# Second-layer attention: queries' rotary sum on POOL, one product per table place, row sums at other heads

## Chip, cores, metric

One core of one Trainium2 chip runs the whole program. The metric is device time in microseconds (us) of one execution, as the median of several. PE is TensorE, DVE is VectorE, ACT is ScalarE, POOL is GpSimd, SP is SyncE, which here only issues DMAs.

## What is computed

Two layers, each `x = x + s * silu(ffn)` with `s` an attention of the normalised input. The change touches only the second layer's attention and the routing work that runs beside it:

```python
# 4 sequences of 512 rows, 256 wide; 16 heads of 128; window 64
h = rmsnorm(layernorm(x)) * norm_w
Q, K, V = lora_proj(h, wq, ...), lora_proj(h, wk, ...), lora_proj(h, wv, ...)
Q = Q * cos + rotate_half(Q) * sin        # the same for K
attn = softmax(Q K^T / sqrt(128) + window mask)
s = lora_proj(attn V, wo, ...) + layernorm(x)
# second ffn: each row goes to 4 of 16 experts
topk_w, topk_ids = top_k(softmax(x @ gate_w.T), 4)
out = shared_expert(x) * sigmoid(...) + sum over the 4 of w * expert(x)
```

For the experts the kernel makes a table: 80 tiles of 128 places sorted by expert, and for each place which row (and which of its 4 choices) stands in it. 2048 rows x 4 choices = 8192 entries; they are brought to their places with one-hot products.

## The kernel before

The program runs in stages that all engines end together; the attention of the second layer is stage 4. There each engine runs its own loop over 64 heads (4 sequences x 16), written out by hand, and engines meet through semaphores. `upto(eng, s, k)` waits until step k of semaphore s was reported, `seen` does the same for counters without lead, and `then_inc` reports. Each engine takes its instructions in the order written.

In turn h of the loop, with the heads that the engines work on at the same time:

- **PE**: `project(h+2)` (L1001; queries, then keys), in some turns `turn_rows` of a tile, an output quarter of an earlier group (L1063), `scores(h+1)` (L1032), `attend(h-1)` (L1051), `turn_probs(h)` (L1041), `values` (L1014).
- **ACT**: `swap(h+2, 0)` and `swap(h+2, 1)` (L1382 and L1383: the rotated halves of queries and keys from PSUM), `output_high`, four exponentials (L1406), `probs_out`, `value_out`; in eight turns the table's L1463.
- **DVE**: `cosine(h+2)` twice (L1808, queries then keys), `masked(h+1)` (four L1828, each with a row minimum; before them, in some turns, the copy or sum of what the table's product left in PSUM), in every second turn `add_output` (L1856), `turned(h+2)` twice (L1814: cosine part + sine part, queries then keys), `output_low` (L1848), `inverse` (L1836), `probs_out` (L1842), and then the turn's extra work.
- **POOL**: `sine(h+2)` (L2166 twice, queries then keys), `normalized(h+1)` (two halves, L2173, then a drain that reports).

The extra work of DVE follows dictionaries of turns. `SUM_AT` says in which turn the first layer's rows of tile t are summed (`summed`: L1730, L1732, L1734, adding 8 loaded parts pairwise) and, one turn later, finished (`finish`: L1740, L1742, L1744, L1746). After the last tile of a sequence come its statistics, and `FOLLOW_AT`, worked out from `SUM_AT`, says in which turns the sequence's four tiles are normalised, turned by PE and split (`rows_low`, L1769). The table's steps run from turn `T0` (two after the last tile's follow-up): counting in `tables(k)`, then eight chunks of eight choices each in turns `T0 + 10` on (`chunk`), the products in `scores` from head `CHUNK0 + 1` on, and the end (from L1961) in turn `T0 + 11 + 8`.

`chunk(c)` makes a one-hot of the tile number for each of eight choices (`ohhi1`, L1891), multiplies it with a code of the column (`ohcol`, L1894), and makes a one-hot of the place in the tile (`ohlo1`, L1895). ACT makes a second scaled copy with the partition's number (`ohtok`, L1463). PE then makes two products for each choice, sixteen in a chunk (L1026 and L1028), all into one PSUM region, which `masked` adds to `idxf` (L1825). All second-layer tiles lie in one buffer called arena in the rows.

Of the kernel before, what the change touches and what calls it, by code (L numbers as in the profile page):

```python
# [8 lines left out]
F16 = mybir.dt.float16  # L9
# [6 lines left out]
P = 128  # L16
T = 2048
NB, SEQ, D = 4, 512, 256
NT = T // P
# [70 lines left out]
def build(nc, io, dbg):  # L90
    ctx = ExitStack()
    with ctx:
# [127 lines left out]
        class Landed:  # L220
# [65 lines left out]
        chosen, counted, counted_rd, exp5_in, exp5_done, chunk_in, tables_done = (  # L286
            sem(n) for n in ("chosen", "counted", "counted_rd", "exp5_in", "exp5_done", "chunk_in", "tables_done"))
# [8 lines left out]
        rope_done = loop_sem("rope_done", "dve", 1, AHEAD)  # L296
# [144 lines left out]
        at_cnt = R6.at  # L441
        CHUNK = 8
        NCHUNK = NT * K1 // CHUNK
        ohhi1 = R6.take(P, CHUNK, XT, dt=F16)
        R6.at = at_cnt
# [10 lines left out]
        colA = R6.take(P, NT * K1)  # L456
# [8 lines left out]
        ohtok = R6.take(P, 2, CHUNK, XT, dt=F16)  # L465
# [82 lines left out]
        SUM_AT = {4: 0, 5: 2, 6: 3, 7: 6, 8: 11, 9: 15, 10: 17, 11: 19, 12: 23, 13: 25, 14: 27, 15: 28}  # L548
# [243 lines left out]
        def _(pe):  # L792
# [225 lines left out]
            def scores(h, u):  # L1018
                upto(pe, sm_done, h - 1)
                for t in tiles_at(FOLLOW_AT, h - 3):  # L1020
                    router(t, ps[4][:, 2 * KW:2 * KW + E1 + 1])
                if 0 <= h - 1 - CHUNK0 < NCHUNK:
                    c = h - 1 - CHUNK0
                    seen(pe, chunk_in, c)
# [198 lines left out]
        def _(act):  # L1223
# [154 lines left out]
            def swap(h, s):  # L1378
                k = 2 * h + s
                upto(act, cos_rd, k)  # L1380
                upto(act, rope_done, k - 2)
                nc.scalar.activation(qk_s[0:64, s], ps[s][64:P, :], ACT.Copy)  # L1382
                nc.scalar.activation(qk_s[64:P, s], ps[s][0:64, :], ACT.Copy).then_inc(swap_rd, 1)  # L1383
# [41 lines left out]
            for h in range(NH):  # L1425
# [108 lines left out]
        def _(dve):  # L1534
# [270 lines left out]
            def cosine(h, s):  # L1805
                upto(dve, proj_mm, 2 * h + s)
                upto(dve, rope_done, 2 * h + s - 2)
# [51 lines left out]
            for h in range(2):  # L1859
                cosine(h, 0)  # L1860
                cosine(h, 1)
                turned(h, h, 0)
                turned(h, h, 1)
# [23 lines left out]
            def chunk(c):  # L1887

                at = slice(CHUNK * c, CHUNK * (c + 1))
                seen(dve, chunk_in, c - 1)  # L1890
# [7 lines left out]
            def tables(k):  # L1898
# [48 lines left out]
                if k == 9:  # L1947
# [6 lines left out]
                    nc.vector.tensor_scalar(colA, iota[:, 0:NT * K1], 1.0, float(P), ALU.add, ALU.mult)  # L1954
                    dve.drain()
                    nc.vector.tensor_copy(loA, loI)
# [23 lines left out]
            for h in range(NH):  # L1980
# [18 lines left out]
                if ahead:  # L1999
                    turned(h + 2, h % 2, 0)  # L2000
                    turned(h + 2, h % 2, 1)
# [106 lines left out]
        def _(pool):  # L2108
# [130 lines left out]
```

## Time and profile before

| | us |
|---|---|
| median of 3 runs | 1355.68 (1355.54 to 1359.92) |
| the profiled execution | 1360.36 |
| its span, first to last instruction | 1358.2 |
| of it, the 64 heads of stage 4 | some 610 |

The profile is one execution. Busy time counts work on an engine; L12 is line 12 of the kernel before. "Idle before" names what ended an engine's wait. `x2` in a timeline row means that two instructions are merged in it. In the chain of waits, "issue" is time in which the engine waited for nothing that the profile shows.

### The profile page before, as it was taken

To read this page: it belongs to the slowest core of one execution; us is meant where nothing else is said; L and a number is where in the kernel's file an instruction comes from. 1 tells how busy PE (TensorE), PEld (TensorE's weight loads), DVE (VectorE), ACT (ScalarE), POOL (GpSimd) and SP (SyncE) were. 2 spreads that over 40 slices of the span, in tenths; PEclk is the share of its full clock that TensorE was granted. 3 is DMA by queue.
4 is the path that set the end of the run, shared out by engine and by line. 5 is a ranking of instruction groups with operands and counts; after the bars stand their busy time and mean duration, and the time that the engine had idled before them with its cause. 6 is when DMAs were issued, how large, how long until landed. Compare 5 with 4: busy or idle time off the path is not lost.

```text
span 1358.2 us, 21102 instructions
## 1 busy us (share of the span) xinstructions
PE 1120.9 (83%) x6075; PEld 709.8 (52%) x6075; DVE 887.2 (65%) x2124; ACT 634.9 (47%) x1680; POOL 600.3 (44%) x577
## 2 busy tenths in 40 slices
PE   4967898617888897887898888898878889788998
PEld 3545343214556665665675555567545455445454
DVE  4586166754887789888777999987443333333575
ACT  1532244434568655855866455566333333333211
POOL 0485365303555454543544544455135565665100
PEclk8978898958999999999999999999888898998999
DMA  9692898580221213120110000020642222222261
GB/s 347 245 322 81 235 275 261 201 275 26 94 93 40 86 32 124 47 78 32 55 41 32 32 1 32 32 96 0 221 105 70 77 73 72 78 81 58 72 204 50
DMA packets 90170, 148.64 MB, mean 109 GB/s; under 512 B 11146, under 2 KB 61965, under 8 KB 87248
## 3 DMA queue, kind: packets, MB, share of 16 engines
q1 hardware_dynamic: 79312, 119.02, 26.4%
q0 software_dynamic: 10752, 28.33, 6.7%
q8 instruction: 52, 0.85, 0.3%
q14 instruction: 54, 0.44, 0.1%
HBM read 104.25 MB, written 45.15 MB: 110 GB/s over the span
## 4 chain that ended last, share of the span: by engine, by line
PE 40%; DVE 18%; issue 13%; ACT 7%; POOL 6%; DMA 4%; another core or an unknown queue 4%; DVEq 3%; ACTq 2%; POOLq 1%; SPq 1%; PEld 0%
PE ps L1173 5%; POOL arena L2166 4%; PE ps L1185 3%; PE ps L1001 3%; PE ps L1183 3%; PE ps L1063 2%; PE ps L822 2%; ACT arena L1383 2%; PE ps L1115 2%; PE ps L884 2%; DVE arena L1842 2%; PE ps L1032 2%; DVE arena L1814 2%; PE ps L1133 2%
## 5 line engine op out<-in xcount | busy, mean ns | idle before, releaser
L2166 POOL TENSOR_TENSOR arena<-arena 128x512 f32<-128x512 f32 x128 | 161.5, 1278 | 226.0 <-ACT arena L1383 225.8
L2173 POOL TENSOR_TENSOR arena<-arena 64x512 f32<-64x512 f32 x128 | 149.7, 1169 | 144.8 <-DVE arena L1836 141.1
L1001 PE MATMUL ps<-arena 128*128 128x512 f16 x768 | 182.1, 388 | 35.3 <-ACT arena L1383 35.3
L1814 DVE TENSOR_TENSOR arena<-arena 128x512 f32<-128x512 f32 x128 | 126.6, 1025 | 33.2 <-POOL arena L2166 31.3
L1001 PEld LDWEIGHTS ps<-arena 128*128 128x128 f16 x768 | 74.1, 99 | 135.7 <-ACT arena L1383 45.5
L2194 POOL DMA_INDIRECT z_d<-wvo,put x80 | 80.9, 1011 | 91.4 <-DVE wvo L2058 69.7
L1382 ACT ACTIVATE arena<-ps 64x512 f32<-64x512 f32 x128 | 76.1, 595 | 93.6 <-DVE arena L1808 89.8
L1406 ACT ACTIVATE arena<-arena 128x192 f32<-128x192 f32 x256 | 112.6, 444 | 2.4 <-DVEq L1831 2.4
L2190 POOL DMA_INDIRECT wvo<-xn_d,idx x80 | 78.0, 975 | 72.3 <-PE ps L1167 35.6
L1063 PE MATMUL ps<-wvo,arena 128*128 128x256 f16 x768 | 97.2, 279 | 13.3 <-DVE arena L1848 12.9
L1014 PE MATMUL ps<-wvo,arena 128*128 128x512 f16 x384 | 94.3, 382 | 16.3 <-ACTq L1361 9.1
L1032 PE MATMUL ps<-arena 128*128 128x192 f32 x512 | 96.3, 331 | 5.6 <-DVE arena L1814 3.8
L1063 PEld LDWEIGHTS ps<-wvo,arena 128*128 128x128 f16 x768 | 75.9, 100 | 35.5 <-DVE arena L1848 17.7
L1173 PE MATMUL ps<-arena,wvo 128*128 x480 | 93.4, 336 | 0.4 <-issue 0.4
L1808 DVE TENSOR_TENSOR arena<-ps,wvo 128x512 f32<-128x512 f32 x128 | 82.8, 681 | 12.6 <-PE ps L1001 10.7
L1051 PE MATMUL ps<-arena 128*128 128x192 f32 (+1 forms) x512 | 87.5, 314 | 4.0 <-DVE arena L1842 4.0
L1828 DVE CUSTOM_DVE_ANT_0 arena<-ps,arena 128x192 f32<-128x192 f32 x256 | 75.7, 351 | 21.7 <-PE ps L1032 21.7
L1051 PEld LDWEIGHTS ps<-arena 128*128 128x128 f32 x512 | 84.8, 190 | 4.8 <-issue 2.5
L1032 PEld LDWEIGHTS ps<-arena 128*128 128x128 f32 x512 | 82.5, 191 | 8.5 <-issue 5.5
L1183 PE MATMUL ps<-arena,wvo 128*128 x160 | 54.7, 426 | 38.8 <-ACTq L1503 38.8
L2044 DVE SCALAR_TENSOR_TENSOR wvo<-ps,wvo 128x256 f16<-128x256 f32 x80 | 34.0, 425 | 75.7 <-ACT wvo L1491 62.2
L1383 ACT ACTIVATE arena<-ps 64x512 f32<-64x512 f32 x128 | 75.5, 590 | 1.5
(286 smaller groups left out, 2205.4 us busy)
## 6 DMA issues: line engine op xcount, KB each, us to landing
arena<-z_d SPq DMA_DIRECT2D x16, 1024.0 KB, 5.9
arena<-wqk_d SPq DMA_DIRECT2D x16, 1024.0 KB, 5.0
arena<-in_wgu SPq DMA_DIRECT2D x32, 384.0 KB
z_d<-wvo SPq DMA_DIRECT2D x8, 1024.0 KB, 4.2
z_d<-wvo SPq DMA_DIRECT2D x2, 4096.0 KB, 25.8
wvo<-z_d SPq DMA_DIRECT2D x16, 512.0 KB, 5.0
arena<-in_wdn SPq DMA_DIRECT2D x32, 192.0 KB
arena<-in_w13T SPq DMA_DIRECT2D x4, 1408.0 KB, 13.1
```

What stands on the lines that cost most here:

```text
L1001: last = pe.matmul(ps[s][:, :], wqk[gg][:, s * DC + c, w, hh * DH:(hh + 1) * DH], hx[bb][:, :, x, c * P:(c + 1) * P], start=(c == 0 and w ...
L1014: last = pe.matmul(ps[2][:, :], hx[bb][:, q, x, c * P:(c + 1) * P], wvo16[:, UNITS + c * NG + g, w], start=(c == 0 and w == x), stop=(c == ...
L1032: last = pe.matmul(ps[3 + q // 2][:, (q % 2) * KW:(q % 2 + 1) * KW], qr[:, u, q * P:(q + 1) * P], kr[:, u, q * P:q * P + KW], start=True, ...
L1051: last = pe.matmul(ps[7][:, k * P:k * P + n], vv[gg][:, k, hh * DH:(hh + 1) * DH], flat(pT[:, k])[:, 0:n], start=(k == 0), stop=(k == TPB ...
L1063: last = pe.matmul(output_bank(n, half)[:, q % 2 * D:(q % 2 + 1) * D], oT[gg][:, x, hh, q * P:(q + 1) * P], wvo16[:, 2 * g + hh // 2, w, h ...
L1173: last = pe.matmul(ps[bank][:, 0:2 * F1], lhs[:, x, c * P:(c + 1) * P], w13[:, bass.ds(e, 1), w, c * 2 * F1:(c + 1) * 2 * F1].rearrange("p ...
L1183: pe.matmul(ps[bank][:, 0:D], h1T[:, u, 0:P], w2a[:, bass.ds(e, 1), :].rearrange("p a d -> p (a d)"), start=start, stop=False)
L1383: nc.scalar.activation(qk_s[64:P, s], ps[s][0:64, :], ACT.Copy).then_inc(swap_rd, 1)
L1406: nc.scalar.activation(pp[u][:, q], sm[:, q], ACT.Exp, bias=mn[:, q:q + 1], scale=-1.0, accum_out=rs[:, q:q + 1])
L1814: nc.vector.tensor_tensor(dst, qk_c[:, s], qk_s[:, s], ALU.add).then_inc(rope_done, 1)
L2166: nc.gpsimd.tensor_tensor(qk_s[:, s], qk_s[:, s], sin, ALU.mult).then_inc(sin_done, 1)
L2173: nc.gpsimd.tensor_tensor(pm[u][rows, at:at + SEQ].rearrange("p (t n) -> p t n", t=TPB), pp[u][rows, :, at:at + P], ri[rows].unsqueeze(2). ...
```

## The change

It has three parts.

1. The sum of cosine part and sine part of the queries is issued by POOL, behind the two sines of that head. DVE keeps the keys' sum and waits for the sine of the keys before it. `rope_done` becomes two semaphores. `normalized` begins with a drain on POOL.
2. In a chunk of the table, eight `tensor_scalar` (one for each choice) compare with the tile number and multiply with a code that holds column and partition in one; the code is the same for each chunk. `ohhi1`, `ohtok`, ACT's L1463 and the second product are gone. What depends on the chunk is added in `masked` through `later`.
3. `SUM_AT` has other turns, and with it `FOLLOW_AT`, `T0` (36 before, 34 after) and `CHUNK0` (48, 46).

```diff
-        SUM_AT = {4: 0, 5: 2, 6: 3, 7: 6, 8: 11, 9: 15, 10: 17, 11: 19, 12: 23, 13: 25, 14: 27, 15: 28}
+        SUM_AT = {4: 0, 5: 2, 6: 4, 7: 6, 8: 9, 9: 11, 10: 13, 11: 15, 12: 17, 13: 22, 14: 24, 15: 26}
...
                     for i in range(CHUNK):
-                        pe.matmul(ps[4][:, 2 * KW:2 * KW + XT], ohlo1[:, c % 2, i], ohtok[:, c % 2, i], start=(i == 0), stop=False,
+                        pe.matmul(ps[4][:, 2 * KW:2 * KW + XT], ohlo1[:, c % 2, i], ohcol[:, c % 2, i], start=(i == 0), stop=(i == CHUNK - 1),
                                   skip_group_check=True)
-                        pe.matmul(ps[4][:, 2 * KW:2 * KW + XT], ohlo1[:, c % 2, i], ohcol[:, c % 2, i], start=False, stop=(i == CHUNK - 1),
-                                  skip_group_check=True)
-                upto(pe, rope_done, 2 * h + 1)
+                upto(pe, rope_done[0], h)
+                upto(pe, rope_done[1], h)
...
-                if 0 <= h - T0 - 10 < NCHUNK:
-                    c = h - T0 - 10
-                    act.wait_ge(picked, c + 1)
-                    nc.scalar.activation(flat(ohtok[:, c % 2]), flat(ohhi1), ACT.Copy, scale=pid[:, 0:1]).then_inc(chunk_in, 1)
...
-            def turned(h, u, s):
-                upto(dve, sin_done, 2 * h + s)
+            def turned(h, u):
+                upto(dve, sin_done, 2 * h + 1)
                 upto(dve, sc_ps, h - 2)
-                dst = qr[:, u] if s == 0 else kr[:, u, WIN:WIN + SEQ]
-                nc.vector.tensor_tensor(dst, qk_c[:, s], qk_s[:, s], ALU.add).then_inc(rope_done, 1)
+                nc.vector.tensor_tensor(kr[:, u, WIN:WIN + SEQ], qk_c[:, 1], qk_s[:, 1], ALU.add).then_inc(rope_done[1], 1)
...
                 if 0 < h - 1 - CHUNK0 < NCHUNK:
+                    c = h - 1 - CHUNK0
+                    nc.vector.tensor_scalar(later, ps[4][:, 2 * KW:2 * KW + XT], 0.0, float(CHUNK * P * c), ALU.is_gt, ALU.mult)
                     nc.vector.tensor_tensor(idxf, idxf, ps[4][:, 2 * KW:2 * KW + XT], ALU.add)
+                    dve.drain()
+                    nc.vector.tensor_tensor(idxf, idxf, later, ALU.add)
...
-                nc.vector.tensor_tensor(ohhi1, iota_bf[:, 0:XT].unsqueeze(1).to_broadcast([P, CHUNK, XT]),
-                                        hiA[:, at].unsqueeze(2).to_broadcast([P, CHUNK, XT]), ALU.is_equal)
-                dve.drain()
-                nc.vector.tensor_tensor(ohcol[:, c % 2], ohhi1, colA[:, at].unsqueeze(2).to_broadcast([P, CHUNK, XT]), ALU.mult)
+                for i in range(CHUNK):
+                    nc.vector.tensor_scalar(ohcol[:, c % 2, i], iota_bf[:, 0:XT], hiA[:, CHUNK * c + i:CHUNK * c + i + 1], colA[:, i:i + 1],
+                                            ALU.is_equal, ALU.mult)
...
                 for s in range(2):
                     upto(pool, swap_rd, 2 * h + s)
                     nc.gpsimd.tensor_tensor(qk_s[:, s], qk_s[:, s], sin, ALU.mult).then_inc(sin_done, 1)
+                upto(pool, sin_done, 2 * h)
+                upto(pool, cos_rd, 2 * h)
+                upto(pool, sc_ps, h - 2)
+                nc.gpsimd.tensor_tensor(qr[:, h % 2], qk_c[:, 0], qk_s[:, 0], ALU.add).then_inc(rope_done[0], 1)
 
             def normalized(h, u):
+                pool.drain()
                 upto(pool, rs_done, h)
```

## Rows read from the trace of the kernel before

**Rows 1.** The page, part 1: busy us, share of span, instructions

```profile
PE 1120.9 (83%) x6075; PEld 709.8 (52%) x6075; DVE 887.2 (65%) x2124; ACT 634.9 (47%) x1680; POOL 600.3 (44%) x577
```

**Rows 2.** Table by stretches: from:to, length, busy us of PE, PEld, DVE, ACT, POOL

```profile
332.00:942.00 610.00, 529.07 (x3253) 371.67 (x3252) 514.74 (x1235) 389.49 (x1011) 302.40 (x250) 0.99 0.16 53
```

**Rows 3.** The same table, stretches of two heads, one table head, one head

```profile
489.21:509.41 20.20, 18.76 (x116) 13.49 (x115) 18.70 (x40) 11.59 (x31) 10.12 (x8) 1.00 0.19 54
812.09:823.09 11.00, 7.54 (x59) 5.44 (x58) 10.60 (x22) 6.41 (x16) 5.06 (x4) 1.00 0.27 95
917.78:925.91 8.13, 8.13 (x52) 5.88 (x51) 5.26 (x17) 5.59 (x15) 4.70 (x5) 1.00 0.00 0
```

**Rows 4.** Chain of waits in order of time: start us, us, what

```profile
335.06 1.28 POOL arena L2166
...
344.85 1.28 POOL arena L2166
...
346.16 0.03 DVE arena L1814
...
347.83 0.62 DVE arena L1814
...
897.77 1.28 POOL arena L2166
```

**Rows 5.** Groups by line, 332 to 942 us, DVE: count, busy us, mean ns, idle

```profile
L1814 DVE TENSOR_TENSOR arena<-arena 128x512 f32<-128x512 f32 x124 | 122.8, 1027 | 30.0 <-POOL arena L2166 28.1 <-issue 0.9
L1808 DVE TENSOR_TENSOR arena<-ps,wvo 128x512 f32<-128x512 f32 x124 | 80.1, 681 | 3.8 <-PE ps L1001 2.5 <-issue 0.7
```

**Rows 6.** Timeline: start us, us, engine, line, what, xcount merged

```profile
491.18 2.50 POOL L2166 TENSOR_TENSOR arena<-arena 128x512 f32<-128x512 f32 x2 [2.96 <-ACT arena L1383]
...
492.48 2.34 DVE L1814 TENSOR_TENSOR arena<-arena 128x512 f32<-128x512 f32 x2
...
498.66 0.43 DVE L1746 BATCH_NORM_STATS2 stat<-x_sb 128x6 f32<-128x256 f32 x1
...
499.01 1.27 DVE L1808 TENSOR_TENSOR arena<-ps,wvo 128x512 f32<-128x512 f32 x2
...
911.67 2.50 POOL L2166 TENSOR_TENSOR arena<-arena 128x512 f32<-128x512 f32 x2 [0.53 <-ACT arena L1383]
...
914.96 1.28 DVE L1814 TENSOR_TENSOR arena<-arena 128x512 f32<-128x512 f32 x2
```

**Rows 7.** Timeline, a sine that began during a DVE add

```profile
455.47 1.64 POOL L2166 TENSOR_TENSOR arena<-arena 128x512 f32<-128x512 f32 x1 [0.98 <-ACT arena L1383]
```

**Rows 8.** Timeline of a table head

```profile
815.61 2.34 DVE L1814 TENSOR_TENSOR arena<-arena 128x512 f32<-128x512 f32 x2 [0.20 <-POOL arena L2166]
...
819.13 1.30 DVE L1891 TENSOR_TENSOR arena<-iota_bf,arena 128x640 f16<-128x640 bf16 x1
...
821.93 1.21 DVE L1895 TENSOR_TENSOR arena<-iota_bf,arena 128x1024 f16<-128x1024 bf16 x1
823.07 1.28 DVE L1808 TENSOR_TENSOR arena<-ps,wvo 128x512 f32<-128x512 f32 x2
...
825.30 2.49 POOL L2166 TENSOR_TENSOR arena<-arena 128x512 f32<-128x512 f32 x2 [3.98 <-ACT arena L1383]
```

**Rows 9.** Timeline, small DVE operations with one input

```profile
789.62 0.20 DVE L1952 TENSOR_SCALAR arena<-arena 128x64 int32<-128x64 int32 x1
789.73 0.19 DVE L1953 TENSOR_SCALAR arena<-arena 128x64 int32<-128x64 int32 x1
...
891.98 0.67 DVE L1961 TENSOR_SCALAR arena<-arena 128x80 int32<-128x80 f32 x1
```

**Rows 10.** Table by stretches: four heads; two with a sum; two without

```profile
353.90:393.24 39.34, 29.22 (x163) 19.44 (x164) 34.94 (x76) 23.19 (x63) 18.84 (x16) 1.00 0.25 81
442.40:463.72 21.32, 19.47 (x125) 14.41 (x125) 18.55 (x50) 11.68 (x32) 8.71 (x7) 1.00 0.26 81
665.71:685.26 19.55, 18.35 (x118) 13.49 (x117) 12.82 (x43) 13.91 (x36) 8.82 (x9) 1.00 0.26 81
```

More of the change, by code:

```diff
@@ L285, in build @@
         kept = [sem(f"kept{b}") for b in range(NB)]
-        chosen, counted, counted_rd, exp5_in, exp5_done, chunk_in, tables_done = (
-            sem(n) for n in ("chosen", "counted", "counted_rd", "exp5_in", "exp5_done", "chunk_in", "tables_done"))
+        chosen, counted, counted_rd, exp5_in, exp5_done, tables_done = (
+            sem(n) for n in ("chosen", "counted", "counted_rd", "exp5_in", "exp5_done", "tables_done"))
         tabs_in = sem("tabs_in")
@@ L295, in build @@
         sin_done = loop_sem("sin_done", "pool", 1, AHEAD)
-        rope_done = loop_sem("rope_done", "dve", 1, AHEAD)
+        rope_done = [loop_sem("rope_q", "pool", 1, AHEAD), loop_sem("rope_k", "dve", 1, AHEAD)]
         v_ps = loop_sem("v_ps", "pe", 1, AHEAD)
@@ L440, in build @@
         mkA = R6.take(P, NT, E1, dt=BF16)
-        at_cnt = R6.at
         CHUNK = 8
         NCHUNK = NT * K1 // CHUNK
-        ohhi1 = R6.take(P, CHUNK, XT, dt=F16)
-        R6.at = at_cnt
         cnt = [R6.take(P, NT, E1) for _ in range(3)]
@@ L455, in build @@
         hiA = R6.take(P, NT * K1)
-        colA = R6.take(P, NT * K1)
+        colA = R6.take(P, CHUNK)
+        later = R6.take(P, XT)
         etf = R6.take(1, XT)
@@ L464, in build @@
         ohlo1 = R6.take(P, 2, CHUNK, P, dt=F16)
-        ohtok = R6.take(P, 2, CHUNK, XT, dt=F16)
         ohcol = R6.take(P, 2, CHUNK, XT, dt=F16)
@@ L1023, in scores @@
                     c = h - 1 - CHUNK0
-                    seen(pe, chunk_in, c)
+                    seen(pe, picked, c)
                     for i in range(CHUNK):
-                        pe.matmul(ps[4][:, 2 * KW:2 * KW + XT], ohlo1[:, c % 2, i], ohtok[:, c % 2, i], start=(i == 0), stop=False,
+                        pe.matmul(ps[4][:, 2 * KW:2 * KW + XT], ohlo1[:, c % 2, i], ohcol[:, c % 2, i], start=(i == 0), stop=(i == CHUNK - 1),
                                   skip_group_check=True)
-                        pe.matmul(ps[4][:, 2 * KW:2 * KW + XT], ohlo1[:, c % 2, i], ohcol[:, c % 2, i], start=False, stop=(i == CHUNK - 1),
-                                  skip_group_check=True)
-                upto(pe, rope_done, 2 * h + 1)
+                upto(pe, rope_done[0], h)
+                upto(pe, rope_done[1], h)
                 for q in range(TPB):
@@ L1380, in swap @@
                 upto(act, cos_rd, k)
-                upto(act, rope_done, k - 2)
+                upto(act, rope_done[s], h - 1)
                 nc.scalar.activation(qk_s[0:64, s], ps[s][64:P, :], ACT.Copy)
@@ L1806, in cosine @@
                 upto(dve, proj_mm, 2 * h + s)
-                upto(dve, rope_done, 2 * h + s - 2)
+                upto(dve, rope_done[s], h - 1)
                 nc.vector.tensor_tensor(qk_c[:, s], ps[s][:, :], cos, ALU.mult).then_inc(cos_rd, 1)
-            def turned(h, u, s):
-                upto(dve, sin_done, 2 * h + s)
+            def turned(h, u):
+                upto(dve, sin_done, 2 * h + 1)
                 upto(dve, sc_ps, h - 2)
-                dst = qr[:, u] if s == 0 else kr[:, u, WIN:WIN + SEQ]
-                nc.vector.tensor_tensor(dst, qk_c[:, s], qk_s[:, s], ALU.add).then_inc(rope_done, 1)
+                nc.vector.tensor_tensor(kr[:, u, WIN:WIN + SEQ], qk_c[:, 1], qk_s[:, 1], ALU.add).then_inc(rope_done[1], 1)
             def masked(h):
@@ L1861, in _ @@
                 cosine(h, 1)
-                turned(h, h, 0)
-                turned(h, h, 1)
+                turned(h, h)
             masked(0)
@@ L1889, in chunk @@
                 at = slice(CHUNK * c, CHUNK * (c + 1))
-                seen(dve, chunk_in, c - 1)
-                nc.vector.tensor_tensor(ohhi1, iota_bf[:, 0:XT].unsqueeze(1).to_broadcast([P, CHUNK, XT]),
-                                        hiA[:, at].unsqueeze(2).to_broadcast([P, CHUNK, XT]), ALU.is_equal)
-                dve.drain()
-                nc.vector.tensor_tensor(ohcol[:, c % 2], ohhi1, colA[:, at].unsqueeze(2).to_broadcast([P, CHUNK, XT]), ALU.mult)
+                for i in range(CHUNK):
+                    nc.vector.tensor_scalar(ohcol[:, c % 2, i], iota_bf[:, 0:XT], hiA[:, CHUNK * c + i:CHUNK * c + i + 1], colA[:, i:i + 1],
+                                            ALU.is_equal, ALU.mult)
                 nc.vector.tensor_tensor(ohlo1[:, c % 2], iota_bf[:, :].unsqueeze(1).to_broadcast([P, CHUNK, P]),
@@ L1953, in tables @@
                     nc.vector.tensor_scalar(hiI, dstI, 7, None, ALU.arith_shift_right)
-                    nc.vector.tensor_scalar(colA, iota[:, 0:NT * K1], 1.0, float(P), ALU.add, ALU.mult)
+                    nc.vector.tensor_scalar(colA, iota[:, 0:CHUNK], 1.0, float(P), ALU.add, ALU.mult)
                     dve.drain()
+                    nc.vector.tensor_scalar(colA, colA, pid[:, 0:1], None, ALU.add)
                     nc.vector.tensor_copy(loA, loI)
@@ L1999, in _ @@
                 if ahead:
-                    turned(h + 2, h % 2, 0)
-                    turned(h + 2, h % 2, 1)
+                    turned(h + 2, h % 2)
                 if h:
```

## Prediction

> **What bounds the kernel now.** The parts of the page came first. PE is busy 83% of the span, but that is a mean over stages [rows 1]. The table by stretches cuts the span into stages: the stretch from 332 to 942 us is the 64 heads of the second layer's attention, the only stage the change touches. It has 610 us, DVE busy 515, PE 529, POOL 302 [rows 2]. Next came stretches of single heads, from one head's first L1808 (the cosine product) to the next's. A head with nothing extra takes 8.13 us, all of it PE: the floor. A head with a row sum and the one after it, which finishes the tile, take 20.20 together, 10.1 each; a head that builds table entries takes 11.0. There DVE is busy 18.70 of 20.20 and 10.60 of 11.00, and PE has gaps [rows 3].
>
> The chain of waits says what DVE waits for there. From the cosine product of the queries it goes DVE L1808, ACT L1382 and L1383 (the two swaps), POOL L2166 (sine of the queries), then DVE L1814, whose second of the pair ends at 347.83 + 0.62 = 348.45 [rows 4]. Behind it on DVE stand L1848, L1842, the tile's work and the next L1808. So the loop closes through DVE, and passes POOL once per head.
>
> The rows that decide are those of L1814. Undisturbed, a pair of them takes 1.28 us, so one takes about 0.68 with the overlap of 0.08 that the pair of L1808 (mean 0.681, same size) shows; but the mean of 124 is 1.027 [rows 5, 6]. (1.027 - 0.68) x 124 = 43 us are lost. A typical pair shows how: POOL's two sines run from 491.18 for 2.50, DVE's two adds start at 492.48 and take 2.34 instead of 1.28. The first add starts behind the first sine, finds POOL in its second sine, and ends about 0.5 after that one's end [rows 6]. L1808, which reads one input from PSUM, keeps 0.681 as a mean [rows 5]. So an add with both inputs in SBUF stands still while POOL works. With 1.06 us lost by each, 43 us is some 40 of 62 heads. It holds the other way too: the sine of 455.47 began while an add was already running, and took 1.64 rather than 1.28 [rows 4, 7].
>
> **Part 1, the queries' add goes to POOL.** DVE loses one L1814 a head, POOL gains one instruction. Its price on POOL is that of the sine, which has the same shape: 1.28 [rows 4]. POOL has room: 302 of 610 us, + 62 x 1.28 = 79. But DVE's remaining add (keys) must wait for the sine of the keys anyway. Call the end of that sine S and the query cosine's start C. In rows bound by DVE the pair before ends at S + 1.15: at 491.18 + 2.50 = 493.68 = S, the adds end at 492.48 + 2.34 = 494.82 [rows 6].
>
> After the change POOL has the queries' add queued directly behind the keys' sine. Its three waits (its own first sine, the cosine, the scores of two heads ago) are all met by then. Are they dealt with while the sine still runs? On DVE they are: L1746 starts at 498.66 and takes 0.43, three waits stand between it and L1808, and L1808 starts at 499.01, before its end [rows 6]. On POOL two sines together take 2.50 against 2 x 1.28, so the second starts some 0.05 before the end of the first, while DVE, which waits for a semaphore, starts 0.03 after it (344.85 + 1.28 = 346.13, L1814 at 346.16) [rows 4, 6]. So I take it that POOL gets in first. Then the keys' add stands still for 1.25 and needs its 0.5: it ends at S + 1.77, 0.62 later than before. The busy time of DVE falls, and its chain grows. In the language of the Trainium skill ("SBUF — State Buffer", "Who interferes with whom") the read port of POOL and of two-input VectorE instructions goes to whichever issues first, for the whole instruction; both orders in rows 6 and 7 agree.
>
> How many heads pay? Those where DVE stands waiting for POOL and the chain goes through the sine. I followed the chain from head to head: 36 sines of queries lie on it with this pattern, the first at 335.06, the last at 897.77 [rows 4]; 8 of these are table heads, counted in part 2. Of the other 28, 25 pay 0.62. In three (sum and row turning in one head) POOL had an idle stretch between the sines which an add used at full speed; there only the keys' add was left at S (the sine of 455.47 ends at 457.11), the pair ended at S + 0.72, and the price is 1.05 [rows 7]. Together 25 x 0.62 + 3 x 1.05 = **+18.7**. In heads at PE's floor DVE arrives after S (914.96 against 911.67 + 2.50 = 914.17) [rows 6]: the add is blocked there as well and ends at S + 1.77 = 915.94, where the pair ended at 916.24, all beside PE work: nothing. Bounds: 28 x -0.47 = -13 if DVE gets in first (below), 36 x 1.05 = +38 if every head pays the dear price.
>
> **Part 2, the table.** Eight heads. DVE loses L1891 and L1894, ACT loses L1463, PE eight of sixteen small products. L1891 takes 1.30 and is mostly standing, behind POOL's first half of L2173; L1894 stands behind the second. From the end of the keys' add (815.61 + 2.34 = 817.95) to the next L1808 (823.07) it is 5.12 us, of that 1.21 L1895 [rows 8]. Added: eight tensor_scalar of 128x80. Two such of 128x64 start 0.11 apart and take 0.20 each, so eight are 7 x 0.11 + 0.20 = 0.97. But they meet POOL's halves too: L1961, one SBUF input, 128x80, took 0.67 behind a half [rows 9]. L1891 ends at 820.43 and needs 0.5 behind POOL, so the first half ends 1.95 after the keys' add [rows 8]. Then either the whole burst and L1895 go through (1.95 + 0.97 + 1.1 = 4.0), or POOL's second half gets in between (+1.05: 5.05). I take 4.5, the middle. ACT's 0.83 delayed the swap: C to S was 4.72 (823.07 to 825.30 + 2.49) [rows 8], it becomes 4.47 as in sum heads (489.21, where the stretch of rows 3 begins with L1808, to 493.68). The head was 4.73 + 1.15 + 5.12 = 11.0; it becomes 4.47 + 1.77 + 4.5 = 10.74: 8 x -0.26 = **-2.1**; bounds 10.24 and 11.29, so -6 to +2.5. The Trainium skill ("VectorE: DVE Perf Modes", "Side-by-side") counts about 150 cycles of start and decode at 0.96 GHz for each instruction; by an estimate from that page eight cost 1.25 us rather than 0.97, and the sum would be 8 x 0.28 = 2.2 us higher. The row has them overlapping, and the row decides. The new product and add in the masking step, some 0.2 each by the tensor_scalar of rows 9, fall where DVE waits for S. PE's and ACT's savings are beside DVE's chain.
>
> **Part 3, the sums spaced.** All twelve stay. One alone costs 20.20 - 2 x 8.13 = 3.9 [rows 3]; one in heads that turn rows 21.32 - 19.55 = 1.8, since those wait anyway [rows 10]. Sums 5 and 6, adjacent, with the free head behind them took 39.34; spaced, the four heads would be twice 20.20 = 40.4: spacing costs 1.0 [rows 3, 10]. Before, sums 8, 12 and 13 lay among the turning heads; after, 8 and 9 do, and 12 at the edge: between 0 and +2. Sum **+2**, bounds -4 (8 and 9 wholly absorbed) and +4. The table starts two heads earlier; its heads were DVE-bound and stay so. Row loads are asked for two sums ahead, now an even 40 us.
>
> **Sum.** 18.7 - 2.1 + 2 = +18.6. The profiled execution took 1360.36 us (span 1358.2 and 2.2 around it), 4.7 over the median of 1355.68. 1360.36 + 18.6 = 1379.0, against the median **1374.3**. Own range of this case: 1362 (half the heads pay, part 2 at its best) to 1386.
>
> **Rivals.** *DVE gets in first* (ends faster). If POOL's three waits take more than about 0.1 us beyond the sine's end, DVE's add starts at S + 0.03 and ends at S + 0.68: 0.47 less than before, in 28 heads -13.2; table heads 4.47 + 0.68 + 4.5 = 9.65, 8 x -1.35 = -10.8; part 3 +2. 1355.7 - 22.0 = 1334. It turns on 0.1 us of order on one engine. Against it: the 0.05 overlap of sine pairs. 13%.
> *The extra is absorbed* (no difference). The chain in DVE heads has other members near: PE is busy 18.76 of 20.20 in them [rows 3]. If only a third of the 0.62 reaches the next head and parts 2 and 3 come to their best (-10): 6.2 - 6 - 4 + 1355.7 = 1352, or 1356 with part 3 at 0. Against it: the chain never leaves DVE, ACT and POOL in a sum head [rows 4]. 10%.
> *More than that*: POOL's L2173 halves come late as well and the tile's sums meet them: the dear price in all 36, 1355.7 + 38 + 2 = 1396. Against it: the query add ends 0.5 before the keys' add, L2173 waits for L1836 well after. 5%.
>
> **Chances.** Forecast 72%, the rivals 13, 10 and 5. Slower by over 0.3% (4 us, about what a measurement of this kernel can tell from no change): 76%; within: 8%; faster: 16%. Range: 1350 to 1387; out of it are the first rival and the last.
>
> **What would show it.** Right: the DVE add of keys has a mean near 1.5 us with a blocked form of 1.74, starting 0.03 after the second sine; POOL shows three instructions in a row of 3.75 together; a sum head takes 11.0 and its follower 10.4; DVE's busy time falls while the stretch grows. Wrong: the keys' add takes 0.68 and POOL's add is the one stretched to 1.6 to 1.9. Part 2: table heads at 10.3 if the burst holds, 11.3 if it is cut, and L1895 blocked or not says which. Part 3 is wrong if sums 8 and 9 cost nothing among the turning heads.

## The result and the profile after

Beside runs of the kernel before on the same chip (median 1357.8 us), the changed kernel takes 1394.58 us as a median of four (1390.53 to 1395.02): 1.026 of the time before, 95% interval 1.0225 to 1.0296. The forecast was slower, 1374.3 with a range of 1350 to 1387: the sign was right, the size half of what came, and the time lies above the range.

The page's part 1, then the table by stretches of the kernel after. Its columns are those of [rows 2]; the first line is the stretch of all heads (from the first masking instruction of head 0 to that of head 63), then a head with a row sum and the head that finishes it, four heads (10 to 13) at the first turned rows, and a table head. The last three columns are PE's mean granted clock, the busy share of the DMA engines and GB/s:

```profile
PE 1136.9 (82%) x6011; PEld 716.1 (51%) x6011; DVE 866.8 (62%) x2123; ACT 628.3 (45%) x1672; POOL 675.8 (49%) x641
```

```profile
330.51:976.77 646.26, 546.89 (x3197) 379.70 (x3198) 496.37 (x1246) 384.17 (x1008) 375.66 (x312) 0.97 0.15 50
599.08:610.07 10.99, 7.92 (x37) 5.19 (x36) 9.40 (x19) 5.58 (x15) 6.68 (x5) 0.85 0.29 97
610.07:620.50 10.43, 10.43 (x67) 7.90 (x66) 8.07 (x19) 6.00 (x16) 5.87 (x5) 0.99 0.00 1
430.92:441.72 10.80, 10.13 (x66) 7.65 (x64) 8.73 (x18) 5.91 (x17) 6.68 (x5) 1.00 0.00 1
441.72:454.17 12.45, 9.11 (x58) 6.67 (x58) 9.45 (x23) 8.43 (x21) 5.92 (x5) 1.00 0.55 190
454.17:466.58 12.41, 10.26 (x55) 6.62 (x54) 9.81 (x24) 7.35 (x20) 6.71 (x5) 0.86 0.04 6
466.58:479.30 12.72, 10.64 (x58) 6.96 (x58) 9.87 (x26) 6.97 (x18) 5.91 (x5) 0.87 0.37 119
849.83:861.18 11.35, 9.01 (x52) 7.09 (x53) 10.44 (x29) 5.58 (x16) 5.85 (x5) 0.85 0.27 92
```

The span grew from 1358.2 to 1392.4, by 34.2 us. Measured between the same two instructions, the heads took 612.80 before and 646.26 after: 33.5 of it. What lies ahead of them grew by 1.2, what lies behind them shrank by 0.4. DVE's busy time fell from 887.2 to 866.8, POOL's rose from 600.3 to 675.8 [rows 1]: the engine that the work was taken from did less, and the heads took longer.

The groups by line for the sines, the keys' sum and the queries' sum (count, busy us, mean ns, idle before):

```profile
L2158 POOL TENSOR_TENSOR arena<-arena 128x512 f32<-128x512 f32 x128 | 160.4, 1270 | 227.2 <-ACT arena L1379 226.9
L1805 DVE TENSOR_TENSOR arena<-arena 128x512 f32<-128x512 f32 x64 | 98.9, 1546 | 80.9 <-POOL arena L2158 80.4
L2162 POOL TENSOR_TENSOR arena<-arena 128x512 f32<-128x512 f32 x64 | 81.2, 1269 | 0.0
```

The mean of DVE's sum went from 1027 ns [rows 5] to 1546, while POOL's own stays at 1269, the price of a sine. The timeline of the sum head in the table above shows one of them:

```profile
601.05 2.50 POOL L2158 TENSOR_TENSOR arena<-arena 128x512 f32<-128x512 f32 x2 [3.58 <-ACT arena L1379]
...
603.50 1.27 POOL L2162 TENSOR_TENSOR arena<-arena 128x512 f32<-128x512 f32 x1
603.58 1.74 DVE L1805 TENSOR_TENSOR arena<-arena 128x512 f32<-128x512 f32 x1 [1.32 <-POOL arena L2158]
605.25 0.68 DVE L1843 SCALAR_TENSOR_TENSOR arena<-ps,arena 128x512 f16<-128x512 f32 x1
```

The sines end at 603.55 (S). POOL's next instruction begins 0.05 before that, DVE's, which waits for a semaphore, 0.03 after it. DVE's stands still until POOL is through and ends at 605.32, which is S + 1.77. The chain of waits of the same head closes through DVE, ACT and POOL as in [rows 4]:

```profile
600.39 0.60 ACT arena L1379
...
601.05 2.51 POOL arena L2158 x2
...
603.58 0.04 DVE arena L1805
...
606.01 0.57 DVE arena L1837
606.58 1.62 DVE arena L1722
...
608.28 1.38 DVE arena L1724
```

### The profile page after: what moved, and what is told of

Same layout as the page of the kernel before. It is cut to its first block, busy times and chain, and to the rows that moved or that the text cites. A ratio compares the mean times of both kernels' runs of the same rounds, so it can differ in the third digit from the quotient of the medians.

```text
span 1392.4 us, 21114 instructions
## 1 busy us (share of the span) xinstructions
PE 1136.9 (82%) x6011; PEld 716.1 (51%) x6011; DVE 866.8 (62%) x2123; ACT 628.3 (45%) x1672; POOL 675.8 (49%) x641
## 4 chain that ended last, share of the span: by engine, by line
PE 40%; DVE 18%; issue 12%; POOL 9%; ACT 5%; DMA 4%; DVEq 4%; another core or an unknown queue 4%; POOLq 2%; ACTq 1%; SPq 1%; PEld 0%
POOL arena L2158 7%; PE ps L1169 5%; PE ps L1181 4%; PE ps L998 3%; PE ps L1179 3%; PE ps L1059 2%; PE ps L819 2%; PE ps L1111 2%; PE ps L1028 2%; DVE arena L1800 2%; PE ps L1011 2%; ACT arena L1379 2%; PE ps L1129 2%; PE ps L881 2%
## 5 line engine op out<-in xcount | busy, mean ns | idle before, releaser
L2158 POOL TENSOR_TENSOR arena<-arena 128x512 f32<-128x512 f32 x128 | 160.4, 1270 | 227.2 <-ACT arena L1379 226.9
L998 PE MATMUL ps<-arena 128*128 128x512 f16 x768 | 185.5, 393 | 34.9 <-ACT arena L1379 34.7
L2170 POOL TENSOR_TENSOR arena<-arena 64x512 f32<-64x512 f32 x128 | 147.9, 1155 | 101.1 <-DVE arena L1831 97.3
L1805 DVE TENSOR_TENSOR arena<-arena 128x512 f32<-128x512 f32 x64 | 98.9, 1546 | 80.9 <-POOL arena L2158 80.4
L1378 ACT ACTIVATE arena<-ps 64x512 f32<-64x512 f32 x128 | 76.1, 595 | 154.6 <-DVE arena L1800 151.2
L1028 PE MATMUL ps<-arena 128*128 128x192 f32 x512 | 102.3, 346 | 12.8 <-DVE arena L1805 10.2
L1028 PEld LDWEIGHTS ps<-arena 128*128 128x128 f32 x512 | 87.7, 201 | 18.9 <-issue 15.2
L1047 PEld LDWEIGHTS ps<-arena 128*128 128x128 f32 x512 | 85.9, 193 | 3.0 <-DVE arena L1843 2.3
L2162 POOL TENSOR_TENSOR arena<-arena 128x512 f32<-128x512 f32 x64 | 81.2, 1269 | 0.0
```

The source lines that it names most:

```text
L998: last = pe.matmul(ps[s][:, :], wqk[gg][:, s * DC + c, w, hh * DH:(hh + 1) * DH], hx[bb][:, :, x, c * P:(c + 1) * P], start=(c == 0 and w ...
L1047: last = pe.matmul(ps[7][:, k * P:k * P + n], vv[gg][:, k, hh * DH:(hh + 1) * DH], flat(pT[:, k])[:, 0:n], start=(k == 0), stop=(k == TPB ...
L1805: nc.vector.tensor_tensor(kr[:, u, WIN:WIN + SEQ], qk_c[:, 1], qk_s[:, 1], ALU.add).then_inc(rope_done[1], 1)
L2170: nc.gpsimd.tensor_tensor(pm[u][rows, at:at + SEQ].rearrange("p (t n) -> p t n", t=TPB), pp[u][rows, :, at:at + P], ri[rows].unsqueeze(2). ...
```

## The experiments

They ran on three chips on which the kernel before takes 1286.60, 1287.47 and 1286.72 us. The 70 us to the first chip lie outside the heads (in the kernels profiled there about 315 us ahead of them instead of 329, about 357 behind them instead of 416), and single heads untouched by an edit have the same length to 0.01. So each run is read twice: as a ratio, which compares medians on one chip, and as the length of the stretch of heads in its one profiled execution, against 612.80 in that of the kernel before.

The second reading has a scatter. The whole change was profiled twice, and its heads take 646.26 and 643.20: head 20 is 11.82 at a mean granted clock of 0.86 in the one and 10.25 at 1.00 in the other, head 29 is 9.79 and 8.12. So a difference of up to 3 us in the heads says little unless single heads show where it lies.

| kernel | us | ratio, 95% interval | heads | against before |
|---|---|---|---|---|
| part 1 alone | 1313.94 | 1.0208 (1.0191 to 1.0225) | 640.38 | +27.6 |
| part 2 alone | 1283.23 | 0.9976 (0.9967 to 0.9986) | 610.59 | -2.2 |
| part 3 alone | 1294.79 | 1.0071 (1.0047 to 1.0095) | 618.78 | +6.0 |
| parts 2 and 3 | 1290.85 | 1.0031 (1.0019 to 1.0042) | 618.96 | +6.2 |
| the whole change | 1317.66 | 1.0245 (1.0228 to 1.0263) | 643.20 | +30.4 |
| part 1, POOL's add after DVE's | 1292.86 | 1.0044 (1.0027 to 1.0062) | 619.63 | +6.8 |
| DVE adds queries, POOL keys | 1284.84 | 0.9983 (0.9969 to 0.9998) | 613.39 | +0.6 |
| part 1, half an add on POOL | 1294.65, one run | | 616.84 | +4.0 |
| part 1, POOL's add behind the halves | 1365.28 | 1.0625 (1.0602 to 1.0649) | 686.19 | +73.4 |
| two sums moved | 1285.63, one run | | 614.76 | +2.0 |
| part 3, swaps ahead of the copies | 1297.65 | 1.0084 (1.0057 to 1.0111) | 623.63 | +10.8 |
| part 2 with the other split | 1283.13 | 0.9973 (0.9962 to 0.9984) | 607.19 | -5.6 |

**The parts one by one.** Four kernels: part 1 alone, part 2 alone, part 3 alone, and parts 2 and 3 without part 1, each made of the lines of the diff of the change; later the whole change on such a chip.

> Before with the first part alone: POOL adds the queries, DVE the keys; the old table, the old sum turns. Theory of the port order: in every head where DVE waits for POOL the keys' add stands 1.26 us behind POOL's add and ends 1.77 after the keys' sine, 0.62 later than the pair did; 28 heads at 0.62 to 1.05 and 8 table heads at 0.62: +18.7 + 5 = +24 over before, keys' add mean 1.5 us. Rival, that the add itself is harmless and the loss of the change sits in the sums and the table: within 5 of before.

> Before with the table alone (eight small tensor_scalar, one product, no ACT copy). Theory that the small operations are cut by POOL's halves: the eight take 2.9 as in the changed kernel, the table head stays at 11.0 less the 0.25 that the ACT copy delayed the swap: -2 to 0. Rival, that the table was a loss of its own (two more operations in the masking step): each table head 0.3 longer, +3.

> Before with the new turns of the sums alone. Theory of the prediction: +2 (bounds -4 and +4). Rival, that sums 8, 9, 10 and 12 in heads that also turn rows are dear by themselves: the heads 427 to 492 us of the changed kernel took 60.8 us where six heads at 9.8 to 10.1 were expected, so +8 to +14 here. Second rival, that they are dear only with the late add: +2 here and the rest appears only with part 1.

> The changed kernel with the queries' add given back to DVE (parts 2 and 3). Port order: all of part 1's loss goes, that is 24 or more below the changed kernel, 1365 to 1370. Rival, that the loss of the whole is in the spacing: stays at 1380 or more.

> The changed kernel again, on the chip of the experiments. If the parts add up there, +27.3 - 3.1 + 8.2 = +32.4 over before; if the three parts worsen each other, more than +36.

Part 1 carries most of it, part 2 is a small gain, and part 3 costs three times the forecast in the heads and four times in time (its profiled execution was the fastest of its four). They nearly add up: 27.6 - 2.2 + 6.0 = 31.4 against 30.4 for the whole, and in time 27.3 - 3.4 + 8.2 = 32.1 against 30.9. So no fourth cost between the parts shows beyond the scatter.

Counted head by head, part 1's 27.6 fall into three. The 28 heads of the chain that the prediction counted grew by 16.2 (forecast 18.7). The eight table heads grew by 0.63 each, 5.0. The other heads, counted at nothing, grew by 6.4: heads 9, 14, 24 and 26 by 2.09, 1.69, 1.09 and 1.04, which turn rows or follow such a head. The 1.69 of head 14 come with a lower granted clock, 0.85 as a mean where the kernel before has 1.00:

```profile
455.95:467.25 11.30, 8.93 (x44) 5.44 (x45) 6.50 (x21) 8.25 (x21) 7.57 (x7) 0.85 0.31 107
```

The three kernels that come next have the same 11.3 there, whatever the order and length of the adds; the last kernel of this section, which also has an add on POOL, has 9.61 at 1.00. So these 1.7 us are none of the port's.

**Is it the order at the port?** Three kernels start from part 1 alone and change who waits for whom, which of the two adds is POOL's, or how long POOL's add is. If the loss comes from DVE standing still behind POOL's add, it must go when POOL waits for DVE, and go as well when POOL adds the keys, so that DVE can add the queries behind the first sine.

```diff
 # POOL's add after DVE's
                 upto(pool, sin_done, 2 * h)
+                upto(pool, rope_done[1], h)
                 upto(pool, cos_rd, 2 * h)
```

> Before with part 1 alone, and POOL's add of the queries made to wait for DVE's add of the keys: the other order at the port, all work as it was. Port order: the keys' add begins 0.03 after the keys' sine, takes 0.68 and ends at S + 0.7, 0.45 before where the pair of before ended; the 64 heads fall by 10 to 15 below before, that is 38 to 43 below part 1 alone. Rival, that DVE's wait for the second sine or POOL's third instruction is the cost whatever the order: like part 1 alone, +27.

The timeline of the head that finishes a tile, POOL's add after DVE's:

```profile
479.08 2.50 POOL L2164 TENSOR_TENSOR arena<-arena 128x512 f32<-128x512 f32 x2 [2.96 <-ACT arena L1384]
...
481.61 0.69 DVE L1814 TENSOR_TENSOR arena<-arena 128x512 f32<-128x512 f32 x1 [1.32 <-POOL arena L2164]
...
482.44 1.27 POOL L2169 TENSOR_TENSOR arena<-arena 128x512 f32<-128x512 f32 x1 [0.86 <-DVE arena L1814]
...
483.16 0.69 DVE L1842 TENSOR_TENSOR arena<-ps,sides 128x512 f32<-128x512 f32 x1 [0.17 <-ACT arena L1389]
...
483.93 2.33 POOL L2177 TENSOR_TENSOR arena<-arena 64x512 f32<-64x512 f32 x2 [0.22 <-issue]
...
485.43 1.11 DVE L1745 TENSOR_TENSOR x_sb<-x_sb,arena 128x256 f32<-128x256 f32 x1
```

DVE's sum now takes 0.69 and ends at S + 0.7, as the first rival of the prediction says. The cost falls from 27.6 to 6.8, so 20.8 of the 27.6 are the order of the two adds, and of the 6.8 that stay 1.7 are head 14. But the gain of that rival doesn't come; my expectation of one was wrong by some 20 us, for two reasons in these lines. L1842 comes early and then waits 0.17 for ACT's L1389 (ACT's `probs_out`, which stands behind its four exponentials): of the 0.47 won only 0.18 are left by then. And POOL's add pushes its normalisation halves (L2177) back, so that they meet other instructions of the tile's finish: the third of them, L1745, takes 1.11 instead of 0.43, the first 0.42 instead of 0.90, and the first three 2.63 together instead of 2.44. Sum heads and their followers are 10.44 and 9.86 instead of 10.38 and 9.81.

```diff
 # DVE adds the queries, POOL the keys
-                upto(dve, sin_done, 2 * h + 1)
+                upto(dve, sin_done, 2 * h)
...
-                nc.vector.tensor_tensor(kr[:, u, WIN:WIN + SEQ], qk_c[:, 1], qk_s[:, 1], ALU.add).then_inc(rope_done[1], 1)
+                nc.vector.tensor_tensor(qr[:, u], qk_c[:, 0], qk_s[:, 0], ALU.add).then_inc(rope_done[0], 1)
...
-                nc.gpsimd.tensor_tensor(qr[:, h % 2], qk_c[:, 0], qk_s[:, 0], ALU.add).then_inc(rope_done[0], 1)
+                nc.gpsimd.tensor_tensor(kr[:, h % 2, WIN:WIN + SEQ], qk_c[:, 1], qk_s[:, 1], ALU.add).then_inc(rope_done[1], 1)
```

> Before with the add split the other way: DVE adds the queries (after the first sine), POOL adds the keys behind the second. Port order: DVE's add queues at the port during the second sine, gets it at S and ends at S + 0.5, 0.65 before the pair of before; POOL's add waits 0.5. 36 heads x -0.65 = -23 at most, less where PE's floor or the probabilities' normalisation, now later, ends the head: -10 to -23. Rival (POOL's load is the cost): +20 or more.

Its timeline, at the same place of a head:

```profile
476.98 2.51 POOL L2164 TENSOR_TENSOR arena<-arena 128x512 f32<-128x512 f32 x2 [2.95 <-ACT arena L1384]
...
478.29 1.75 DVE L1814 TENSOR_TENSOR arena<-arena 128x512 f32<-128x512 f32 x1
479.57 1.60 POOL L2168 TENSOR_TENSOR arena<-arena 128x512 f32<-128x512 f32 x1
...
481.06 0.69 DVE L1842 TENSOR_TENSOR arena<-ps,sides 128x512 f32<-128x512 f32 x1 [0.34 <-ACT arena L1389]
```

Here DVE's add waits inside POOL's second sine, comes next, and it is POOL's add that is stretched, to 1.60. The timeline says DVE is through 0.55 after S, and the heads cost +0.6 instead of +27.6. Of the expected 10 to 23 us little is gained, for L1842 waits 0.34 for ACT: a sum head is 10.36 instead of 10.38. The 0.6 has two heads at a lower clock in it, 14 (+1.7) and 39 (+1.05 at 0.76 instead of 0.87); without them it is -2.1, and the time is 0.9983 of before, an interval that ends just under 1. The order of the adds accounts for nearly all of the loss, and what is late next is ACT, with L1389 behind its exponentials.

```diff
 # half an add on POOL (the other half of the columns is left out)
-                nc.gpsimd.tensor_tensor(qr[:, h % 2], qk_c[:, 0], qk_s[:, 0], ALU.add).then_inc(rope_done[0], 1)
+                nc.gpsimd.tensor_tensor(qr[:, h % 2, 0:SEQ // 2], qk_c[:, 0, 0:SEQ // 2], qk_s[:, 0, 0:SEQ // 2], ALU.add).then_inc(rope_done[0], 1)
```

> Part 1 alone, with POOL's add on half of the columns (256 of 512; the other half of the turned queries is left out and stays zero). Port order: the add takes 0.67, the keys' add stands 0.65 instead of 1.25 and ends at S + 1.17, where the pair of before ended: the heads within 3 of before. Rival, a fixed price of the new wait or of one more POOL instruction: +20 or more stays.

The two adds in the timeline of that kernel:

```profile
484.05 0.73 POOL L2169 TENSOR_TENSOR arena<-arena 128x256 f32<-128x256 f32 x1
484.13 1.20 DVE L1815 TENSOR_TENSOR arena<-arena 128x512 f32<-128x512 f32 x1 [1.33 <-POOL arena L2165]
```

DVE's add takes 1.20 where it took 1.74: it shrinks by 0.54 as POOL's add shrinks by 0.54. So no fixed price of an add on POOL shows; DVE waits out its length. It ends at S + 1.2, near the pair's S + 1.15, and sum heads and table heads grow by 0.08 or 0.09 each. Of the 4.0 in all 1.7 are head 14. It is one run.

**POOL's add still later.** The queries' add has time until PE's scores of that head. So it can go behind POOL's normalisation halves.

```diff
+            def turned_queries(h):
                 upto(pool, sin_done, 2 * h)
...
+                if h + 2 < NH:
+                    turned_queries(h + 2)
```

> Part 1 alone, POOL's add of the queries placed behind the two halves of the normalisation. The keys' add of DVE is then free at S and ends at S + 0.7; ACT's exponentials (0.2 to 0.3 behind) cap that gain; POOL's add now meets the last of DVE's sum or finish. Theory: heads within 4 of before, no gain; rival, that the keys' add alone decides: -10.

Neither came: it cost +73. The groups by line of that kernel:

```profile
L1033 PE MATMUL ps<-arena 128*128 128x192 f32 x512 | 110.7, 365 | 117.4 <-issue 85.8 <-POOL arena L2170 29.2 <-DVEq L1831 2.4
...
L1809 DVE TENSOR_TENSOR arena<-ps,wvo 128x512 f32<-128x512 f32 x128 | 82.2, 682 | 70.4 <-POOL arena L2170 63.6 <-PE ps L1001 5.9 <-issue 0.9
...
L1814 DVE TENSOR_TENSOR arena<-arena 128x512 f32<-128x512 f32 x64 | 46.4, 725 | 97.6 <-POOL arena L2164 97.6
```

DVE's add is free now (725 ns), but the add (L2170) reads the cosine part, and that tile has one buffer. The next head's cosine product on DVE waits for it (63.6 us), and PE's scores wait for the queries that it makes (29.2 us; the 85.8 put down to "issue" are at least in part the same wait, for one of them ends at 518.77 and the add before it at 518.70). A buffer that is free early in the kernel before is held longer when its reader moves.

**Part 3: where do the sums cost?** First only the two sums that the prediction had absorbed by turning heads are moved, in the kernel before.

```diff
-        SUM_AT = {4: 0, 5: 2, 6: 3, 7: 6, 8: 11, 9: 15, 10: 17, 11: 19, 12: 23, 13: 25, 14: 27, 15: 28}
+        SUM_AT = {4: 0, 5: 2, 6: 3, 7: 6, 8: 9, 9: 11, 10: 17, 11: 19, 12: 23, 13: 25, 14: 27, 15: 28}
```

> Before with only two sums moved: 8 from turn 11 to 9, 9 from turn 15 to 11. Theory that a sum is cheap only where the head before it was free or turning for long, and dear in the first turning heads: the two cost 2.05 and 2.6 before and 3.7 each at the new turns, heads +3. Rival, that the turning heads absorb sums (the prediction): the heads fall by 2 to 4.

Heads 10 to 13 of the kernel before, the first that turn rows, and heads 16 to 18, in the table by stretches:

```profile
423.67:463.69 40.02, 37.33 (x236) 27.32 (x235) 30.88 (x82) 28.67 (x74) 19.82 (x17) 1.00 0.20 63
481.34:510.57 29.23, 27.70 (x168) 19.38 (x166) 26.74 (x56) 15.82 (x45) 14.56 (x12) 1.00 0.13 38
```

The same heads with the two sums moved, and head 11 of these by itself:

```profile
406.79:452.71 45.92, 39.02 (x236) 27.75 (x235) 37.11 (x90) 29.09 (x75) 21.61 (x17) 0.96 0.27 90
470.35:495.71 25.36, 25.36 (x158) 18.59 (x157) 19.05 (x49) 15.40 (x44) 13.57 (x12) 1.00 0.01 2
417.47:430.20 12.73, 9.42 (x49) 5.97 (x50) 9.10 (x24) 9.33 (x23) 5.38 (x5) 0.87 0.52 187
```

They aren't absorbed. Turn 11 has a sum before and after, so in effect one sum goes from turn 15 to turn 9. Heads 16 to 18 give back 3.9, the price of a lone sum (my expectation had 2.6, since it left out head 18, which falls from 10.39 to 9.10). Heads 10 to 13 take 5.9 more, with a lower clock in head 11. The other heads stay as they were, and the rest is the 2.0. Part 3 alone has the same two sums in these four heads and the same length, 45.84.

PE's wait for ACT's copies of the turned rows in heads 10 to 13, in the kernel before, with two sums moved, and in part 3 alone (us in total, times, longest):

```profile
PE ps L1014 <- ACTq L1361: 1.3, 1, 1.3
PE ps L1014 <- ACTq L1361: 6.0, 2, 3.5
PE ps L1014 <- ACTq L1361: 7.6, 3, 3.5
```

PE's values use the PSUM bank of the turned rows, and stand until ACT has copied these out. So in these heads PE waits 4.7 and 6.3 more where the heads grow by 5.9. Over all heads the same wait is 9.1 before and only 9.5 in part 3 alone, since heads 25 to 27, which paid it before, no longer do: it goes with the dear heads, and doesn't by itself make up the 6.0. ACT has the swap of the queries ahead of the copies, and the swap waits for DVE's cosine product, which comes late in a head with a sum. If ACT's order is the cause, it should help to let ACT do both swaps first, so that the loop through DVE doesn't wait for the copies:

```diff
 # part 3, swaps ahead of the copies
-                for t in tiles_at(FOLLOW_AT, h - 1):
-                    turned_rows(t, 2)
                 if h + 2 < NH:
                     swap(h + 2, 1)
+                for t in tiles_at(FOLLOW_AT, h - 1):
+                    turned_rows(t, 2)
```

> The new sum turns alone (+6 in the heads, +8 in all), with ACT reading both swaps before it copies the rows that PE turned (before: queries' swap, rows, keys' swap). If sums in turning heads are dear because these copies put the keys' sine 1.0 later in the loop through DVE, the six heads 10 to 14 and 18, 19 fall by 0.6 to 1.0 each and the heads are at +2 or less over before. Rival, that it is DVE's own load (sum, rows, best four): stays at +6.

It doesn't help. The time is 1.0084 of before against 1.0071 for part 3 alone, each inside the other's interval. Heads 12 and 14 shrink (11.38 to 9.77, 10.99 to 9.62) and heads 11 and 13 grow (11.78 to 13.81, 12.08 to 13.33); the four together are 46.5 instead of 46.2. The +10.8 in the heads against +6.0 are for the most part head 20, 14.18 here and 10.26 in part 3 alone, and compare the slowest of this kernel's four runs with the fastest of the other's. The timeline of head 20:

```profile
526.72 2.72 PE L1014 MATMUL ps<-wvo,arena 128*128 128x512 f16 x6 [3.20 <-ACTq L1361]
...
529.23 4.36 PE L1001 MATMUL ps<-arena 128*128 128x512 f16 x12
```

PE waits 3.20 for the copies, and then its matmuls run slowly: six of values take 2.72 instead of 1.46, twelve of the projection 4.36 instead of 2.75. The granted clock, 1.00 as a mean in most heads, is 0.76 in this one: behind the idle time PE was granted the lower of its two levels, 1.2 GHz, for a while. So a wait of PE's can cost twice. In the kernel after, heads 12 and 13 in the table of the section before have a mean clock of 0.86 and 0.87. That the copies hold up PE is shown by the waits; that this other order of ACT's cures it is refuted. How much of part 3's cost is waiting and how much the clock stays open, for the clock falls in different heads in two executions of one schedule: heads 11 and 12 are 12.44 and 12.42 in one execution of the whole change and 13.78 and 11.10 in the other, the same together, but head 20 is 11.82 in the one and 10.25 in the other.

**A version that beats both.** Part 2, the split with keys on POOL, and the sums at their old turns:

> The table of the change, the old sum turns, and the add split the other way (DVE the queries, POOL the keys). Heads: table -2.2, split +0.6: -1.6 against before. Rival: a saving that shows only together, since ACT's copy and DVE's add both delay the table heads: -4 or more.

1283.13 us, 0.9973 of before (0.9962 to 0.9984), 34.5 us less than the whole change (1317.66) on the same chip. Part 2 alone gives 0.9976, so the split adds nothing that the time can show. Of the 5.6 us that the heads lost, 1.7 are one head (39) that ran at a clock of 1.00 here and 0.87 in the profile of before; the other 3.9 are the table's 2.2 and a gain of 1.7 that fits the split's once heads 14 and 39 are left out, but is within the scatter.

## Why the prediction was right in sign and wrong in size

**What bounds the kernel, and part 1's mechanism: right, to the hundredth.** POOL first by 0.05, DVE blocked for 1.74, the end at S + 1.77, sum heads of 11.0 (10.99) and followers of 10.4 (10.43), a mean near 1.5 (1.546), DVE's busy time down while the stretch grows: all as written, and the kernel with POOL's add behind DVE's shows that the order does it. The rule of the Trainium skill named in the prediction ("SBUF — State Buffer", "Who interferes with whom") holds here in both directions, 1.74 for DVE behind POOL and 1.60 for POOL behind DVE. What was wrong is the size of three terms.

**Who pays for part 1: mis-sized by 3.9.** Outside the table heads part 1 costs 22.6, forecast 18.7. The three heads priced at 1.05 paid 0.46, 0.39 and 0.66, and the heads off the chain, most of them turning rows and taken as free because their chain lay on PE or ACT in the kernel before, paid 6.4. Of that 1.7 are the clock of head 14. The rest is the step that failed: the chain before says where the time went before, not how close behind it DVE's loop stood in the heads that it passed by.

**Part 2: mis-sized by 4.9.** A table head was to take 4.47 + 1.77 + 4.5 = 10.74; it took 4.47 + 1.77 + 5.11 = 11.35. The last term failed, "the middle" between a whole burst and a cut one. The timeline of the table head that starts at 849.83, and below it POOL's second half in the table head of [rows 8]:

```profile
852.53 1.74 DVE L1805 TENSOR_TENSOR arena<-arena 128x512 f32<-128x512 f32 x1 [0.70 <-POOL arena L2158]
...
855.04 2.19 POOL L2170 TENSOR_TENSOR arena<-arena 64x512 f32<-64x512 f32 x2 [1.31 <-DVE arena L1831]
855.46 2.86 DVE L1885 TENSOR_SCALAR arena<-iota_bf,arena 128x80 f16<-128x80 bf16 x8
858.24 1.21 DVE L1887 TENSOR_TENSOR arena<-iota_bf,arena 128x1024 f16<-128x1024 bf16 x1
859.38 1.27 DVE L1800 TENSOR_TENSOR arena<-ps,wvo 128x512 f32<-128x512 f32 x2
```

```profile
819.80 1.53 POOL L2173 TENSOR_TENSOR arena<-arena 64x512 f32<-64x512 f32 x1
```

The eight take 2.86 from first start to last end. Singly, the first waits out POOL's first half (0.65), the second takes 0.29, the third, which starts at 856.25, is caught by POOL's second half (begun at 856.13) and takes 1.02, and the others last 0.29 each and start 0.21 apart. So the burst is cut at its third instruction, and the 5.11 are the bad end of the range, 5.05. A whole burst was hardly to be had: in both kernels POOL's second half begins 0.06 after the end of its first. Before, it met L1891, which had 0.6 to go, and waited (1.53 instead of 1.04); among instructions of 0.29 it is soon through (1.10).

The burst's own length was wrong as well. Undisturbed, eight take about 7 x 0.21 + 0.29 = 1.76, not 0.97, which came from L1952 and L1953 [rows 9]: these have constants as operands where L1885 has two columns of a tile. (L1948 of the kernel after, with one column and 128x8, starts 0.14 ahead of its follower; L1744, with constants and 128x4, 0.08.) The estimate from the Trainium skill ("VectorE: DVE Perf Modes", "Side-by-side"), 1.25 for the eight from start and decode alone, was nearer than the row that I preferred and is still too low; the measurement decides. In the cut burst this error is made up by two others, for the first half ended 0.15 earlier than put down and the second cost 0.7 instead of 1.05. Of the two rewards forecast, only ACT's copy came: a table head shrank from 11.00 to 10.73 with part 2 alone, by 0.27 where that term was to give 0.25 (4.72 to 4.47). DVE's own work bought nothing: from the end of the keys' sum to the next cosine it is 5.11, as the 5.12 before.

**Part 3: mis-sized by 4.** Forecast +2 (bounds -4 to +4), measured +6.0 in the heads (8.4 on top of part 2, 618.96 - 610.59) and +8.2 in time. The step that failed: the sum at turn 11, behind two turning heads, cost 1.8 [rows 10], and that price was taken for any sum among turning heads. A second one at turn 9 costs 5.9, and the place that it left, turn 15, gives back 3.9. The difference of 5.9 to 1.8 is as large as the whole miss; how the other moved sums balance stays open. "Part 3 is wrong if sums 8 and 9 cost nothing" had the sign the wrong way about. What the prediction's view of the loop lacked, by the waits in these heads, is the PSUM bank that turned rows and values share, and the clock that PE is granted after waiting for it; that these two are the whole reason isn't shown, and the one cure tried didn't help.

**The sum.** 3.9 + 4.9 + 4 = 12.8 on top of 18.6 is 31.4, which is what the parts alone add up to in the heads; the whole change measured 30.4 there on one chip and 33.5 on the first. Against the paired runs of before the time rose by 36.8 (1394.58 - 1357.8), of which the profiled runs show 34.2 and the rest is scatter between runs; the base itself was 2.1 above the 1355.68 that the forecast started from. All three errors have one sign, and in each a cost was taken as hidden or halved that came in full. *More than that* (1396) has nearly the right time by chance: its price of 1.05 in all 36 heads of the chain wasn't paid, 28 of them grew by 0.58 as a mean (16.2 / 28).

## What to carry to other kernels

Moving a two-input SBUF operation from VectorE to POOL frees little or nothing when both engines need their operands at the same moment: read who starts first at the end of the releasing instruction, and let POOL take the operation whose inputs come last, so that the stretched one is POOL's (here 0.9983 of before instead of 1.0208). Price an operation that the trace lacks by a row with the same kinds of operands, not only about the same size, and where a range is set by whether a burst is cut, take the cut as likely if it is longer than the time until the other engine's next instruction. A price read in one place of a loop (a sum at turn 11) isn't the price of the same work two turns earlier. When a member of the loop gets shorter, look for the wait right behind it (here for ACT, 0.17 to 0.34 us away) before counting the gain.

## What the runs showed of the hardware

- A VectorE instruction at work in a queue of like ones doesn't keep POOL out: POOL's second half began at 856.13, while the second of eight `tensor_scalar` was ending, and the third took 1.02 instead of 0.29.
- At the end of a sine, POOL's next instruction came 0.08 ahead of a VectorE add that had waited for the semaphore (603.50 and 603.58). A VectorE add that was already standing behind the same sine came ahead of POOL's next, which took 1.60 instead of 1.27.
- `tensor_scalar` of 128x80 with two columns as operands: 0.29 long and 0.21 apart; with constants, 128x64 and int32, 0.20 and 0.11 [rows 9].
- The granted clock in a head can differ between two executions of one schedule: head 20 took 11.82 us at a mean of 0.86 and 10.25 at 1.00.
- The kernel before took 1357.8 us on one chip and 1286.6 to 1287.5 on three others; heads that no edit touches have the same length on all, and what differs outside them stays open.
